# A fused decoder layer on one core: decay exponentials taken per head with a bias, DVE's linked small operations made steps of their own, gelu in three sessions, and a new order on every engine

## What is computed

```python
x = layernorm(x + attn(x))
x = layernorm(x + xattn(x, ctx, ctx))
x = layernorm(x + ffn(x))

# attn, 16 heads of 8 features
Q = linear(cat(q_in, conv3(q_in)));  K = linear(cat(k_in, conv3(k_in)));  V = linear(x)
tau   = sigmoid(conv1(gelu(depthwise_conv3(x))))
delta = sigmoid(conv1(gelu(depthwise_conv3(x))))
attn  = softmax(Q @ K.T / sqrt(8) * tau[q] + delta[k]) @ V @ out_w

# xattn, 4 heads of 32 features
log_f = logsigmoid(fg);  G = cumsum(log_f)
log_D = G[s] - G[t] + ig[t] for t <= s, else -inf
D     = exp(log_D - max_t log_D)
C     = (q @ k.T / sqrt(32)) * D
C     = C / (max(|sum_t C|, exp(-max_t log_D)) + 1e-6)
hn    = per-head layernorm(C @ v) * (1 + ln_weight)

# ffn: x and the weight are scaled in blocks of 32 and rounded to a 6-bit grid, then multiplied
```

## Time and profile before

| | |
|---|---|
| median of three runs | 234.24 us (232.49 to 236.56) |
| the profiled execution | 234.09 us |
| its span on the core | 232.3 us |
| PE busy | 206.4 us (89%), of which 17.8 us are `warm` |
| DVE / ACT / POOL busy | 169.7 / 128.6 / 115.2 us |

### The profile page before, as it was taken

The page is one execution under the profiler, slowest core; times in us unless marked ns, Lnnn a source line. Parts: engine busy times, 40 slices in busy tenths (PEclk is TensorE's granted clock), DMA queues, the critical chain, the costliest instruction groups (busy, mean ns, idle before and its releaser), DMA issues.

```text
span 232.3 us, 6553 instructions
## 1 busy us (share of the span) xinstructions
PE 206.4 (89%) x2377; PEld 137.6 (59%) x2377; DVE 169.7 (73%) x429; ACT 128.6 (55%) x365; POOL 115.2 (50%) x225
## 2 busy tenths in 40 slices
...
DMA packets 11311, 8.43 MB, mean 36 GB/s; under 512 B 2736, under 2 KB 10384, under 8 KB 11280
## 3 DMA queue, kind: packets, MB, share of 16 engines
...
## 4 chain that ended last, share of the span: by engine, by line
DVE 35%; PE 35%; issue 17%; POOL 7%; ACT 5%; POOLq 0%; DVEq 0%; ACTq 0%
PE bankPV L847 9%; PE score L633 6%; DVE u L995 5%; DVE u L996 4%; DVE nm L1054 4%; PE bankY L911 2%; PE score L639 2%; DVE z L1185 2%; PE bankP L704 2%; PE bankP L774 2%; PE score L645 2%; POOL qm L296 2%; DVE z L1164 1%; DVE mT L1157 1%; DVE hn L1140 1%
## 5 line engine op out<-in xcount | busy, mean ns | idle before, releaser
L1054 DVE TENSOR_REDUCE nm<-score 128x8 f32<-128x1024 f32 x32 | 38.8, 1219 | 9.3 <-PE score L633 9.3
L507 ACT ACTIVATE prob<-score 128x1024 f32<-128x1024 f32 x32 | 32.5, 1019 | 22.9 <-PE score L645 22.7
L633 PE MATMUL score<-km,qf 32*128 32x512 f32 x128 | 34.1, 642 | 1.2 <-DVE nm L1054 1.2
L639 PE MATMUL score<-qm,kf 32*128 32x512 f32 x128 | 34.3, 645 | 0.1
L466 ACT ACTIVATE u<-u,db 128x512 f32<-128x512 f32 x16 | 11.3, 719 | 19.0 <-DVE u L996 19.0
L645 PEld LDWEIGHTS score<-nmT,sel 32*128 32x128 bf16 x256 | 10.3, 95 | 16.7 <-issue 16.5
L296 POOL TENSOR_SCALAR km<-kf,mcol 128x512 f32<-128x512 f32 x16 | 13.9, 888 | 10.8 <-DVE kf L1031 5.6
L847 PE MATMUL bankPV<-prob,vz 128*32 128x128 f32 x512 | 18.7, 289 | 0.0
L917 PE MATMUL bankPV<-maskb,identb 128*128 128x512 bf16 x73 | 17.8, 380 | 0.0
L847 PE MATMUL bankPV<-prob,ez 128*32 128x128 f32 x512 | 17.3, 275 | 0.0
L627 PE MATMUL bankP<-xTp,wT 128*128 128x512 f32 x36 | 16.8, 602 | 0.4 <-ACT dth L476 0.4
...
## 6 DMA issues: line engine op xcount, KB each, us to landing
...
```

Source lines behind the costliest of these rows:

```text
L507: nc.scalar.activation(prob[:, i % 2, k:k + 2, :].rearrange("p k s -> p (k s)"), sc[:, 512 * k:512 * (k + 2)], ACT.Exp, scale=SQ_SCALE).th ...
L633: ins = mm(sc[:, 512 * k:512 * (k + 1)], qf[r, n, :], km[r, n % (2 * CB)].rearrange("p j s -> p (j s)"), start=True, stop=True)
L639: mm(sc[:, 512 * k:512 * (k + 1)], kf[r, n, :], qm[r, n % (2 * CB)].rearrange("p j s -> p (j s)"), start=True, stop=False)
L1054: nc.vector.tensor_reduce(nm[:, i % 3, J * k:J * (k + 2)], sc[:, 512 * k:512 * (k + 2)].rearrange("p (h s) -> p h s", s=S), AX_X, ALU.max, ...
```

## The change

1. `dm` on POOL keeps the triangle and loses the add (L393) and its wait for g. `dec` on ACT is for all groups one exponential per head and sequence, 8 of 128x128 for a group of two, with g as the bias.
2. The linked chains of DVE become steps: `gb`, `ga`; `na`, `nb`, `nrm`; `v0`, `vs`; `za`, `z2`; `ba`, `bn`, `be`; `q0`, `q1`, `q2`, `q3`, `qa`. Each has its own semaphore. `hn8`, `st` are doubled so that two groups can be under way.
3. The absolute value of the sum of a row is made by ACT (`ha`), and DVE's instruction for it (L1140) goes.
4. Gelu comes in three sessions of 7, 5 and 4 instructions, so there are two more table loads.
5. All five order tables are new. `warm` falls from 73 to 41 matmuls.

```diff
 PE_ORDER = """
-    tx.0 ab.0 hw.0 mT.0 mT.1 wT.0 tx.1 del.0 tx.2 wT.1 tau.0 K.0 del.1 Q.0 Q.1 tx.3 del.2 aa.0 Q.2 gw.0 aa.1 tau.1 cg.0 nmT.0 ow.0 v1.2 nmT.1 K.1 edT.0
...
+    tx.0 ab.0 mT.0 mT.1 tx.1 wT.0 wT.1 tx.2 tx.3 K.0 Q.0 cT.0 gw.0 hw.0 K.1 tau.0 cg.0 tau.1 del.0 aa.0 cm.0 ow.0 edT.0 rc.0 aa.1 V.0 nmT.0 cm.1 V.1 v1.2
...
 ACT_ORDER = """
...
-    edx.2 eY.0 nmT.1 edc.0 eX.0 edc.1 eY.1 edc.2 eX.1 cT.0 nmT.2 cm.0 eY.2 cm.1 rec.0 nmT.3 eX.2 y1s.0 sq1.0 nmT.4 eY.3 l1.0 eX.3 gelu.1 geT.6 geD.6 geT.7
...
+    xT.0 geD.0 xT.1 geT.0 xT.2 xT.3 geT.1 cT.0 geT.2 geT.3 geD.1 thT.0 geD.2 thT.1 thD.0 exp.0 cm.0 edx.0 edc.0 nmT.0 cm.1 eY.0 eX.0 nmT.1 gelu.1 geD.3
+    geT.4 geD.4 geT.5 thD.1 geD.5 exp.1 eY.1 edx.1 nmT.2 eX.1 edc.1 rec.0 eY.2 nmT.3 y1s.0 sq1.0 yT.0 eX.2 l1.0 eY.3 nmT.4 eX.3 gelu.2 geD.6 geT.6 thT.2
...
@@ POOL
                 elif name == "dm":
                     w = NH * GR[i][1]
                     pool.wait_ge(spread[i % 2], 16 * (i // 2 + 1))
-                    pool.wait_ge(g_done, i + 1)
                     t = dec[:, i % 2, 0:w * S].rearrange("p (h s) -> p h s", s=S)
-                    link(nc.gpsimd.affine_select(out=t, in_=t, compare_op=ALU.is_ge, fill=MASKED, base=0,
-                                                 pattern=[[0, w], [1, S]], channel_multiplier=-1))
-                    nc.gpsimd.tensor_tensor(t, t, g[:, i % 2, 0:w].unsqueeze(2).to_broadcast([P, w, S]), ALU.add).then_inc(dm_done, 1)
+                    nc.gpsimd.affine_select(out=t, in_=t, compare_op=ALU.is_ge, fill=MASKED, base=0,
+                                            pattern=[[0, w], [1, S]], channel_multiplier=-1).then_inc(dm_done, 1)
@@ ACT
-                elif name == "dec" and i not in BY_ROWS:
-                    w = NH * GR[i][1]
-                    act.wait_ge(dm_done, i + 1)
-                    t = dec[:, i % 2, 0:w * S]
-                    nc.scalar.activation(t, t, ACT.Exp).then_inc(dec_done, 1)
                 elif name == "dec":
-                    act.wait_ge(ld_ps, BY_ROWS.index(i) + 1)
+                    if i in BY_ROWS:
+                        act.wait_ge(ld_ps, BY_ROWS.index(i) + 1)
+                    else:
+                        act.wait_ge(dm_done, i + 1)
                     act.wait_ge(g_done, i + 1)
                     if i >= 2:
                         act.wait_ge(cc_done, i - 1)
-                    for h in range(NH):
-                        ins = nc.scalar.activation(dec[:, i % 2, S * h:S * (h + 1)], pb[:, S * h:S * (h + 1)], ACT.Exp, bias=g[:, i % 2, h:h + 1])
+                    for k in range(NH * GR[i][1]):
+                        t = dec[:, i % 2, S * k:S * (k + 1)]
+                        ins = nc.scalar.activation(t, pb[:, S * k:S * (k + 1)] if i in BY_ROWS else t, ACT.Exp, bias=g[:, i % 2, k:k + 1])
                     ins.then_inc(dec_done, 1)
+                elif name == "ha":
+                    w = NH * GR[i][1]
+                    act.wait_ge(hs_done, i + 1)
+                    if i >= 2:
+                        act.wait_ge(na_done, i - 1)
+                    nc.scalar.activation(ha[:, i % 2, 0:w], hs[:, i % 2, 0:w, DH], ACT.Abs).then_inc(ha_done, 1)
@@ DVE
+                elif name == "na":
+                    w = NH * GR[i][1]
+                    dve.wait_ge(ha_done, i + 1)
+                    dve.wait_ge(em_done, i + 1)
+                    nc.vector.scalar_tensor_tensor(hn8[:, i % 2, 0, 0:w], em[:, i % 2, 0:w], NRM_MAX, ha[:, i % 2, 0:w],
+                                                   ALU.min, ALU.max).then_inc(na_done, 1)
...
                 elif name == "nrm":
-                    hv = hs[:, i % 2, 0:w, DH]
-                    h0, h1, h2 = (hn8[:, k, 0:w] for k in range(3))
-                    link(nc.vector.scalar_tensor_tensor(h0, em[:, i % 2, 0:w], NRM_MAX, hv, ALU.min, ALU.max))
-                    link(nc.vector.scalar_tensor_tensor(h1, hv, -1.0, h0, ALU.mult, ALU.max))
-                    link(nc.vector.scalar_tensor_tensor(h1.rearrange("p (h v) -> p h v", v=nb), h1.rearrange("p (h v) -> p h v", v=nb), NRM_MAX,
-                                                        se[:, i % YR, 0:nb].unsqueeze(1).to_broadcast([P, NH, nb]), ALU.min, ALU.add))
-                    nc.vector.scalar_tensor_tensor(h2, h1, LN_EPS, h1, ALU.mult, ALU.mult).then_inc(nrm_done, 1)
+                    w = NH * GR[i][1]
+                    dve.wait_ge(nb_done, i + 1)
+                    h1 = hn8[:, i % 2, 1, 0:w]
+                    nc.vector.scalar_tensor_tensor(hn8[:, i % 2, 2, 0:w], h1, LN_EPS, h1, ALU.mult, ALU.mult).then_inc(nrm_done, 1)
...
+                elif name == "q2":
+                    n4 = 4 * GR[i][1]
+                    dve.wait_ge(q1_done, i + 1)
+                    if i >= 2:
+                        dve.wait_ge(xd_done, i - 1)
+                    nc.vector.tensor_scalar(qs8[:, i % 2, 1, 0:n4], qs8[:, i % 2, 0, 0:n4], FP8_STEP / FP6_MAX, FP8_STEP * 1e-30,
+                                            ALU.mult, ALU.max).then_inc(q2_done, 1)
```

More of the change, by code:

```diff
@@ new lines @@
+    Q.1 v2.2 nmT.1 Q.2 v1.3 del.1 pv.0 tau.2 nmT.2 v2.3 edT.1 pv.1 v1.4 nmT.3 y1.0 v2.4 yT.0 v1.5 nmT.4 pv.2 v2.5 gF.0 pv.3 v1.6 del.2 nmT.5 del.3 MT.0
+    tau.3 K.2 v2.6 edT.2 K.3 v1.7 nmT.6 V.2 y1.1 v2.7 V.3 pv.4 v1.8 gF.1 cT.1 pv.5 v2.8 cm.2 nmT.7 y1.2 qk.0 cm.3 nmT.8 pv.6 v1.9 edT.3 Q.3 v2.9 MT.1
+    hst.0 gF.2 v1.10 yT.1 pv.7 v2.10 nmT.9 V.4 y1.3 qk.1 MT.2 V.5 pv.8 v1.11 nmT.10 hst.1 dT.0 v2.11 gF.3 cT.2 ffn.0 v1.12 cT.3 nmT.11 pv.9 v2.12 cm.4
+    yT.2 y1.4 yT.3 qk.2 pv.10 nmT.12 v1.13 hst.2 dT.1 v2.13 gF.4 cm.5 ffn.1 v1.14 cm.6 nmT.13 pv.11 v2.14 MT.3 V.6 y1.5 qk.3 pv.12 nmT.14 V.7 v1.15 V.8
@@ new lines @@
+    geT.7 geD.7 thD.2 nmT.5 thD.3 thT.3 exp.2 eY.4 rec.1 em.0 edx.2 dec.0 edc.2 eX.4 edx.3 eY.5 nmT.6 y1s.1 sq1.1 eX.5 l1.1 eY.6 cT.1 rec.2 eX.6 cm.2
+    nmT.7 y1s.2 sq1.2 cm.3 nmT.8 dec.1 l1.2 eY.7 edc.3 eX.7 em.1 hs.0 hq.0 ha.0 eY.8 yT.1 rh.0 rec.3 eX.8 nmT.9 y1s.3 sq1.3 std.0 em.2 dec.2 l1.3 eY.9
+    nmT.10 hs.1 dT.0 hq.1 ha.1 eX.9 cT.2 sq3.0 nmT.11 eY.10 rh.1 cT.3 rec.4 eX.10 yT.2 std.1 cm.4 y1s.4 dec.3 yT.3 sq1.4 nmT.12 eY.11 l1.4 hs.2 dT.1 hq.2
+    ha.2 eX.11 cm.5 sq3.1 cm.6 eY.12 rh.2 nmT.13 rec.5 eX.12 y1s.5 em.3 dec.4 std.2 nmT.14 sq1.5 eY.13 yT.4 l1.5 dT.2 hs.3 hq.3 ha.3 eX.13 cm.7 sq3.2
@@ L604, in _ @@
                     act.wait_ge(z3_done, i + 1)
+                    act.wait_ge(be_done, i + 1)
                     if i >= 2:
@@ L1153, in _ @@
+                    nc.vector.scalar_tensor_tensor(hn8[:, i % 2, 3, 0:w], hn8[:, i % 2, 6, 0:w], 1.0 / DH, hn8[:, i % 2, 2, 0:w],
+                                                   ALU.mult, ALU.add).then_inc(vs_done, 1)
+                elif name == "za":
                     nb = GR[i][1]
```

163 lines of the change are left out of this document (89 added, 74 removed).

## The result

The changed kernel took 222.78, 229.4, 233.16 and 222.73 us, median 226.1, against a median of 234.1 us before. Ratios in this document are of the executions within 1.5% of their kernel's fastest, each against the kernel before: here 0.9565 (95% interval 0.9508 to 0.9622), 4.35% faster. The four executions differ in the mean clock that TensorE was granted: 0.972 in both of 222.8 us, 0.952 and 0.924 in the other two; this turns out to matter. The profiled execution is one of 222.78 us, with a span of 220.8.

A forecast was written before the change was run, and what follows sets the result against it. PE was taken to bound the full stretch, DVE the front and tail. Gains of 3.2 (front), 0 (full stretch) and 3.4 (tail) make 6.6 us off 234.09: 227.5 us, range 221 to 233.

The forecast's parts named there:

- Rival 2: More than the sum: front 6, idle regained 2, tail 4, giving 222.1 us; chance 0.17.
- First maximum 35.5 us: Front: fewer taps ahead, less `gw` and a POOL wait, start the first DVE maximum 4.7 us sooner, from 40.21 us.
- `mY.4` done 4 to 6 us sooner: Sign to look for on DVE: the maxima of the fifth sequence finish 4 to 6 us sooner.
- The lead is still some 4.5 us when PE becomes full: Front to `v2.4`: moved taps fit DVE's idle time, keeping 4.5 us; less 1.3 us of table loads, 3.2 us net.
- Rival 4: PE slower in the tail: fewer `warm`, clock falls, some 3 us of useful work doubles, 230.5 us; chance 0.07.
- The additional gelu session: ACT between `eX.0` and `eY.1`: another hole of 6.2 us in the exponentials, 1.3 us of it on PE's path.
- I take 0 for this stretch: Full stretch: PE's regained idle set against waits for ACT, net 0; ends -3 and +8.5 us.
- Tail, 60% of 5.7 = 3.4 us: After 194.97 us: four savings on DVE sum to 5.7 us, 60% taken as 3.4; ends 0 and 5.7.
- Term (a): Tail: POOL's add no longer stops two DVE instructions, saving 1.6 us.
- Term (c): Tail: about five small DVE links per group, in four groups, get a foreign instruction between them, saving 2.4 us.
- Rival 3: ACT becomes what PE waits for, at `eX`/`eY` behind longer decays and two holes: 240.7 us; chance 0.07.
- No DVE instruction of 2 us, ACT 141, POOL 101: Signs in the profile: ACT busy near 141 us, POOL near 101, and no DVE instruction of 2 us.

## Why the prediction was right and where it was not

The forecast was 227.5 us (221 to 233), faster. The ratio times 234.1 is 223.9 us, the profiled execution took 222.8: right in sign and within the range, some 4 us too high, and by its steps it was right for partly wrong reasons. Rival 2 is nearest in its number, 222.1 us, and wrong in its parts: it had 6 us in the front, 2 regained and 4 in the tail, and the spans show 1.5, 5.7 and 4.3. That the range held is in part luck, as the miss of the front and the miss of the full stretch have opposite signs.

- *First maximum 35.5 us*: 35.84. The taps and the additional wait for POOL (1.7 us, measured 2.01) were priced well. But the sign that hung on it, `mY.4` done 4 to 6 us sooner, failed: 1.5 us (72.94 to 71.41).
- *"The lead is still some 4.5 us when PE becomes full", 3.2 us net*: 1.5 us. The clock is one half of what was missing: with it held up `v2.4` started 3.7 us sooner than before (70.54 to 66.88), and the fall at 38 us took 2.1 of them. The other half is that the profiled execution of before had falls of its own ahead of `v2.4`. Against the old tables with the new code, which had none there and began `v2.4` at 69.09 us, the front's lead is only 2.2 us, so the premise that the same work is done and the lead of 4.5 us is kept was wrong as well. Rival 4 had looked for this in the tail alone.
- *The additional gelu session*: a hole of 6.2 us as worked out (53.45 to 59.67), with no idle of PE in it. The second one is 10.05 us (78.28 to 88.33), and there PE is idle 2.1 us; from 90 us to the last `pv` it is idle only 1.6 us.
- *"I take 0 for this stretch"*: 5.7 us, beyond the step's own end of 3. This is the step that failed. It counted PE's idle time as all that an order could regain, and the idle time hardly changed (5.7 to 5.4 us). Some 1.7 us are the clock's fall at the last `pv` (3.4 us at half), and 4 us are the order, since from the start of `v2.4` to the last `pv` the old tables with the new code took 122.6 us at a clock of 1.0 and the new tables, padded, 118.7 (66.88 to 185.55). The larger part of that, up to 2.8 us, is the second halves of `v` that had waited inside busy time for a maximum on DVE. Its other half, that ACT's 12.9 us are hidden because ACT is idle 24%, is true of this order only as it stands: of doubled decays some 10 of 11 us came through, by the estimate above.
- *Tail, 60% of 5.7 = 3.4 us*: 4.3 us. The sum was near and its terms were not. With the add gone and the old order kept the tail was 38.0 us, and with L1140 gone too 39.0 (3.4 us of it at half), not under 37.3; only with the order did it fall, and undoing the order alone costs 3 to 4 us. I had priced DVE's chain alone. Term (a), the stop of DVE under the add, is real, but its price depends on what waits: nothing in the old order, and in the new one a wait of PE with the clock's fall behind it. Term (c), the links, stays unmeasured.
- *Rival 4, PE slower in the tail, 0.07*: the clock is real as a cost, and the executions of 229.4 and 233.2 us had a mean clock of 0.952 and 0.924; neither has a trace, so where it fell is open. 41 paddings kept it up in the profiled tail. In the tails of the kernels with an add, with adjacent steps or without padding it stood at 0.58 to 0.81, and they took 6 to 12 us more, instead of the 3 I gave it.
- *Rival 3, ACT as the bound, 0.07*: not in this kernel, but one doubling of its decays away from it.
- *No DVE instruction of 2 us, ACT 141, POOL 101*: all so (139.7 and 100.5). DVE 165 was too much: 156.3. The new decay alone brought DVE from 169.7 to 165.2 us, the rest of the code to 159.8 in the old order, and the new order to 156.3. The last `pv`, at 187.75 us, came sooner than the 190 to 193 I gave it.

What stays open: what a link costs, how the 4 us of the full stretch divide among the tables, and whether some other order suits the old decay.
